# A state-space block and a product-key expert layer on one core: three more scaled rows on TensorE, and the stages dealt out anew

## The chip, the cores and the metric

The kernel runs on one core of one Trainium2 chip, in fp32. The metric is device time in microseconds of the whole program, median of three runs. Engines are named PE (TensorE), DVE (VectorE), ACT (ScalarE), POOL (GpSimd) and SP (SyncE).

## The reference

4096 tokens of width 512 go through two layers, each added to its input and layer-normed.

```python
x = _layernorm(x + attn(x))     # a Mamba-2 block
x = _layernorm(x + ffn(x))      # a product-key expert layer

# attn: u @ W_in -> z, xBC, dt; causal conv of 4 taps and silu; then
y, _ = ssd(x * dt[..., None], A * dt, B, C, 64)   # 16 heads of 64, state 128
y = (y + x * D) * silu(z)                         # x * D: the skip term
out = rmsnorm(y) * norm_scale @ W_out

# ffn: h = silu(x @ W_up.T + b_up) @ W_down.T + b_down   (512 -> 2048 -> 256)
sim = keys . (h @ W_q.T)                # 8 heads, 2 x 64 keys
scores, idx = top_k(sim, 8)             # then the 8 best of the 8 x 8 sums
indices                                 # 64 expert rows of each token
z = silu((h . down_embed[indices]) * softmax(sc))
out = sum over the 64 of z * up_embed[indices]
```

## The kernel before, in words

The tokens are 32 tiles of 128. For each tile every engine has an order written out by hand: a function `tile(i, first, ahead)` in the PE, ACT and DVE blocks. In one pass it does three things at once: the expert rows of tile i-1 that are left (`old`), the first expert rows of tile i (`new`), and the state-space block of tile i+1 (the calls under `ahead`), with the up, down and key projections of tile i between them. The engines meet only at semaphores.

**Expert rows.** One pick is one row of 768 numbers for each of the 128 tokens (256 of down_embed, 512 of up_embed). POOL gathers the 64 picks of a tile in order by indirect DMA (L275) into a ring of 13 slots; pick k+13 waits until pick k is used. The picks are in 22 groups, `GROUPS`; 0 to 3 are `new`, 4 to 21 `old`. For each pick DVE makes the dot with h (L1167), and ACT the coefficient by a Silu (L664). What then happens depends on the pick's letter. A `D` row is weighed by DVE (L1181), multiplied by its coefficient and added to a running sum, two groups later (`LAG`). A `P` row is scaled by ACT into one of 4 buffers (L673, 128x512) and added on PE by four transposes that accumulate in a bank (L506). At the end of a tile ACT copies this bank (`sum_out`, L681), PE turns it back (L514) and DVE adds it to its own sum (L1212) and norms it.

**The stages that the change moves.** On ACT: `xbc_copy` (L689), `inputs` (L701, L704: the three parts of the turned projection, each with a first tap), `turn_x1` (L793: the copy of the transposed x1, for which the up projection waits), `up_copy` and `up_silu` (L800, L806), `conv_silu` (L710), `masked_steps` (L726), `gates` (L736), `decays` (L741 to L750), `soft_exp` (L816), `skip_term` (L717: 8 scalings by D, which PE's y_diag waits for), `end_decay` (L758: xdec, for which DVE's scan output and PE's state_in wait), `state_decay` (L766), `turn_y` (L775), `gated_squares` and `gated_rms` (L780, L784), `back_sqrt` (L820) and `deviation` (L789). On PE: `up_proj` (L463), `turn_up` (L470), `down_proj` (L479), `z_proj` (L360), `y_off` (L397), `y_diag` (L413, L416), `turn_y` (L432), `out_proj` (L442) and `turn_back` (L514). On DVE: `convolve` (L1012), `private` (L1085: the vector h), `top_half`, `find_half` (L1091, L1097), `find_pairs` (L1124), `numbers` (L1146, which gives POOL its indices), `scaled_x` and `masked_products` (L1020 to L1029), `scan_out` (L1038) and `residual` (L1068, which waits for the last of out_proj by `op_mm`).

## Time and profile before

| | us |
|---|---|
| median of three runs (lowest, highest) | 3131.76 (3126.43, 3133.64) |
| the profiled execution | 3120.3 |
| its span, first to last instruction | 3118.5 |
| DVE busy in the span | 2770.7 |
| PE busy | 2628.5 |
| ACT busy | 2325.9 |
| POOL busy (2048 gathers) | 2062.9 |
| weighings on DVE, L1181 (1312 in the main form) | 988.0 |
| scaled rows on ACT, L673 (672 = 32 x 21) | 446.8 |

The span holds a start before the first tile, 32 tiles and an end in which the last tile's rows are used. Shares of busy time are means over stretches with different limits. An engine's idle time counts where another waits for it, so the rows of one tile in order of time tell more than the sums. The mean granted TensorE clock is 0.931 of full speed, where 1.00 is 2.4 GHz.

### The profile page before, as it was taken

What the parts mean: (1) busy time and instruction counts of PE and PEld (TensorE: products, weight loads), DVE (VectorE), ACT (ScalarE), POOL (GpSimd) and SP (SyncE); (2) the same over time, 40 slices, a digit from 0 to 9 for tenths busy, and PEclk for the clock granted to TensorE, in tenths of its full rate; (3) what the DMA queues carried; (4) which work ended last, traced back from release to release, by engine and by line L of the source; (5) the groups of instructions that cost most, each with busy time, mean ns of one, the idle gap of its engine ahead of it and who ended that gap; (6) DMA issues with size and microseconds to landing.
All of it is one profiled execution on the core that took longest, in us unless ns stands there. A gap on an engine that the chain in (4) does not pass through costs nothing.

```text
span 3118.5 us, 42958 instructions
## 1 busy us (share of the span) xinstructions
PE 2628.5 (84%) x10688; PEld 1613.2 (52%) x10688; DVE 2770.7 (89%) x10160; ACT 2325.9 (75%) x6674; POOL 2062.9 (66%) x2056
## 2 busy tenths in 40 slices
PE   7988888888888888888888888889888888888862
PEld 4455555555555555555555555555555555555531
DVE  3489899989999999999999999999999998999986
ACT  3477887777887777787777788777788777788753
POOL 0067676666676676676667667667667666667676
PEclk9999999999999999999999999999999999999975
DMA  8078888888888888888888888888888888888897
GB/s 284 26 264 279 283 285 268 280 291 279 279 289 273 273 299 280 281 289 269 268 296 281 281 285 282 263 281 294 282 279 289 272 275 292 279 278 290 271 310 271
DMA packets 189850, 856.65 MB, mean 275 GB/s; under 512 B 36192, under 2 KB 39392, under 8 KB 189088
## 3 DMA queue, kind: packets, MB, share of 16 engines
q0 software_dynamic: 163840, 805.44, 77.0%
q1 hardware_dynamic: 19104, 34.87, 3.2%
q10 hardware_dynamic: 6656, 13.60, 1.2%
q8 instruction: 85, 1.39, 0.2%
q14 instruction: 165, 1.35, 0.1%
HBM read 845.38 MB, written 8.39 MB: 274 GB/s over the span
## 4 chain that ended last, share of the span: by engine, by line
DVE 35%; PE 33%; ACT 11%; issue 9%; DMA 6%; POOL 6%; POOLq 0%; ACTq 0%; DVEq 0%; SPq 0%
PE bank L463 15%; DVE ring L1167 9%; DVE bank L1181 9%; PE bank L479 7%; POOL ring L275 6%; DMA ring<-embed,idx 6%; PE bank L338 3%; DVE i L1097 3%; ACT xc L704 3%; DVE v L1091 2%; DVE xdt L1138 2%; ACT scaled L673 2%; PE bank L470 2%; ACT coef L664 2%; DVE place L1124 1%
## 5 line engine op out<-in xcount | busy, mean ns | idle before, releaser
L275 POOL DMA_INDIRECT ring<-embed,idx x2048 | 2061.6, 1007 | 1040.9 <-issue 517.0
L1181 DVE SCALAR_TENSOR_TENSOR bank<-ring,coef,bank 128x512 f32<-128x512 f32 x1312 | 988.0, 753 | 8.8 <-ACT coef L664 1.4
L1167 DVE SCALAR_TENSOR_TENSOR ring<-ring,hcur 128x256 f32<-128x256 f32 x2048 | 815.4, 420 | 58.0 <-DMA ring<-embed,idx 55.7
L664 ACT ACTIVATE coef<-prob,zp 128x1 f32<-128x1 f32 x2048 | 455.6, 293 | 237.0 <-DVE ring L1167 235.8
L463 PE MATMUL bank<-w_up,zs 128*128 128x512 f32 x1024 | 509.4, 650 | 97.5 <-ACT zs L793 93.9
L506 PE MATMUL bank<-cst,scaled 128*128 128x128 f32 x2688 | 410.9, 305 | 171.9 <-ACT scaled L673 171.8
L506 PEld LDWEIGHTS bank<-cst,scaled 128*128 128x128 f32 x2688 | 351.2, 159 | 245.9 <-ACT scaled L673 213.3
L673 ACT ACTIVATE scaled<-ring,coef 128x512 f32<-128x512 f32 x672 | 446.8, 714 | 10.4
L463 PEld LDWEIGHTS bank<-w_up,zs 128*128 128x128 f32 x1024 | 206.6, 210 | 335.4 <-issue 233.9
L1012 DVE SCALAR_TENSOR_TENSOR xc<-raw,taps,xc 128x128 f32<-128x128 f32 x960 | 265.5, 348 | 90.7 <-ACT xc L704 90.6
L338 PE MATMUL bank<-w_in,ut 128*128 128x512 f32 (+1 forms) x768 | 289.7, 528 | 47.1 <-ACT seg L689 47.1
L800 ACT ACTIVATE h<-bank 128x512 f32<-128x512 f32 x128 | 76.4, 597 | 246.3 <-PE bank L463 246.3
L442 PE MATMUL bank<-w_out,xdec 128*128 128x512 f32 x512 | 252.6, 639 | 4.3 <-ACT xdec L775 4.3
L338 PEld LDWEIGHTS bank<-w_in,ut 128*128 128x128 f32 x768 | 142.0, 191 | 184.9 <-issue 108.1
L360 PE MATMUL bank<-w_in,ut 128*128 128x512 f32 x512 | 228.0, 599 | 4.4 <-ACT xc L704 4.4
L479 PE MATMUL bank<-w_down,seg 128*128 128x256 f32 x1024 | 231.6, 379 | 0.0
L479 PEld LDWEIGHTS bank<-w_down,seg 128*128 128x128 f32 x1024 | 189.6, 190 | 23.1
L1167 DVE DVE_READ_ACCUMULATOR ring<-ring,hcur 128x1 f32 x2048 | 171.3, 84 | 0.0
L360 PEld LDWEIGHTS bank<-w_in,ut 128*128 128x128 f32 x512 | 98.3, 192 | 128.5 <-issue 128.5
L442 PEld LDWEIGHTS bank<-w_out,xdec 128*128 128x128 f32 x512 | 102.6, 213 | 113.0 <-issue 105.1
L806 ACT ACTIVATE seg<-bank,bup 128x128 f32<-128x128 f32 x512 | 145.8, 373 | 14.2 <-PE bank L470 14.2
L726 ACT ACTIVATE seg<-cst,cur 128x128 f32<-128x128 f32 x512 | 155.6, 391 | 0.0
(150 smaller groups left out, 3764.4 us busy)
## 6 DMA issues: line engine op xcount, KB each, us to landing
ring<-embed,idx POOLq DMA_INDIRECT x2048, 4.6
ring<-uT SPq DMA_DIRECT2D x4, 2048.0 KB, 14.3
ut<-uT SPq DMA_DIRECT2D x32, 256.0 KB, 6.7
zs<-u SPq DMA_DIRECT2D x32, 256.0 KB, 6.2
out<-acc SPq DMA_DIRECT2D x32, 256.0 KB, 5.0
w_up<-W_upT ACTq DMA_DIRECT2D x1, 4096.0 KB, 12.8
w_in<-W_in ACTq DMA_DIRECT2D x1, 2560.0 KB, 17.2
w_in<-W_in ACTq DMA_DIRECT2D x1, 2048.0 KB, 21.7
```

What stands on the lines that cost most here:

```text
L275: pool.indirect_dma_start(out=ring[:, k % RING, :], out_offset=None, in_=embed, in_offset=bass.IndirectOffsetOnAxis(ap=idx[:, half, k:k + ...
L338: m = pe.matmul(bank[XR_BANKS[part]][:, 0:hi - lo], uT_v[:, k, :], w_in[:, k, DI + lo:DI + hi], start=(k == 0), stop=(k == KD - 1))
L360: m = pe.matmul(bank[Z_BANKS[b]][:, :], uT_v[:, k, :], w_in[:, k, b * BANK:(b + 1) * BANK], start=(k == 0), stop=(k == KD - 1))
L442: m = pe.matmul(bank[OP][:, :], yT[:, c * P:(c + 1) * P], w_out[:, c, :], start=(c == 0), stop=(c == KX - 1))
L463: m = pe.matmul(bank[UP_BANKS[b]][:, :], x1T[:, k, :], w_up[:, k, b * BANK:(b + 1) * BANK], start=(k == 0), stop=(k == KD - 1))
L479: m = pe.matmul(bank[DOWN][:, 0:DP], h1T[:, c, :], w_down[:, c, :], start=(c == 0), stop=(c == KU - 1))
L506: m = pe.matmul(bank[SUM][:, c * P:(c + 1) * P], scaled[:, (NPR * t + n) % BUFS, c * P:(c + 1) * P], ident, start=(n == 0 and c == 0), sto ...
L664: m = act.activation(coef[:, k:k + 1], prob_v[:, k:k + 1], ACT.Silu, scale=zp[:, k:k + 1])
L673: act.activation(scaled[:, n % BUFS, :], ring[:, k % RING, DP:ROW], ACT.Copy, scale=coef[:, k:k + 1])\
L1012: m = dve.scalar_tensor_tensor(out=xc[:, c, :], in0=raw[:, c, j:j + P], scalar=taps[:, c, j:j + 1], in1=xc[:, c, :], op0=ALU.mult, op1=ALU ...
L1167: m = dve.scalar_tensor_tensor(out=ring[:, k % RING, 0:DP], in0=ring[:, k % RING, 0:DP], scalar=1.0, in1=hcur[:, :], op0=ALU.mult, op1=ALU ...
L1181: dve.scalar_tensor_tensor(out=total if n == len(DVE_ROWS) - 1 else running[:, :], in0=ring[:, k % RING, DP:ROW], scalar=coef[:, k:k + 1], ...
```

## The change

`GROUPS` has 24 letters P instead of 21, in other places. On all three engines stages and groups change places. `gates` becomes `gate`, one call for each half, and `skip_term` waits for `hist_ok` too. The table of groups, and PE's part:

```diff
-GROUPS = ("DD", "PPPD", "DD", "DDD", "PPD", "DDD", "DD", "DDD", "PDDD", "DDD", "DDD", "DDDD", "PDD", "PPPD", "PP", "PDD", "PPPP", "D", "DDD", "PPPD", "D", "PDD")
+GROUPS = ("DD", "PPPD", "DD", "DDD", "PPD", "DDD", "PD", "DDD", "PDDD", "DDD", "DDD", "PDDD", "PDD", "PPPD", "PP", "PD", "PPPPD", "D", "PDD", "PPPPD", "D", "DD")
...
                     turn_xbc(i + 1, False, 0)
                     turn_xbc(i + 1, False, 1)
                     turn_xbc(i + 1, False, 2)
+                old(4, 5)
                 turn_x1(i)
-                old(4, 5, 6)
+                old(6)
                 up_proj(i, 0, first, ahead)
                 up_proj(i, 1, first, ahead)
+                old(7)
                 turn_up(i, 0)
                 up_proj(i, 2, first, ahead)
                 turn_up(i, 1)
-                old(7, 8)
                 up_proj(i, 3, first, ahead)
                 turn_up(i, 2)
+                old(8)
                 down_proj(i, 0, first, ahead)
+                old(9, 10)
                 turn_up(i, 3)
-                old(9)
                 down_proj(i, 1, first, ahead)
-                old(10)
                 down_proj(i, 2, first, ahead)
                 down_proj(i, 3, first, ahead)
+                old(11)
                 turn_h(i, ahead)
-                old(11, 12)
+                old(12)
                 key_scores(i, 0)
                 key_scores(i, 1)
                 if ahead:
                     z_proj(i + 1, 0)
+                old(13)
+                if ahead:
                     z_proj(i + 1, 1)
-                old(13)
-                if ahead:
                     step_sums(i + 1, 0)
                     step_sums(i + 1, 1)
                     step_sums(i + 1, 2)
                     step_sums(i + 1, 3)
                     turn_x(i + 1)
-                old(14, 15)
+                old(14, 15, 16, 17)
                 if ahead:
                     y_off(i + 1, False)
-                old(16, 17)
-                if ahead:
                     y_diag(i + 1, False, 0)
+                old(18)
+                if ahead:
                     y_diag(i + 1, False, 1)
-                old(18, 19)
+                old(19, 20, 21)
                 if ahead:
                     state_in(i + 1)
                     turn_y(i + 1)
-                old(20, 21)
-                if ahead:
                     out_proj(i + 1, False, 0)
+                new(0)
                 if not first:
                     turn_back(i - 1)
-                new(0)
+                new(1, 2, 3)
                 if ahead:
                     out_proj(i + 1, False, 1)
-                new(1, 2, 3)
```

ACT's part:

```diff
             def skip_term(i):
 
                 act.wait_ge(xc_ok, i + 1)
+                act.wait_ge(hist_ok, i + 1)
                 for c in range(KX):
...
                     xbc_copy(i + 1, 1)
                     xbc_copy(i + 1, 2)
                     inputs(i + 1, 0)
-                old(5)
+                old(5, 6)
+                turn_x1(i)
                 if ahead:
                     inputs(i + 1, 1)
-                turn_x1(i)
-                old(6)
-                if ahead:
                     inputs(i + 1, 2)
-                save_x1(i, first)
                 old(7)
                 up_copy(i, 0)
                 old(8)
+                up_silu(i, 0)
+                save_x1(i, first)
                 up_copy(i, 1)
-                up_silu(i, 0)
+                up_silu(i, 1)
                 up_copy(i, 2)
-                up_silu(i, 1)
                 old(9)
                 up_copy(i, 3)
                 up_silu(i, 2)
...
                 turn_h(i)
                 if ahead:
                     masked_steps(i + 1, range(0, NH // 4), False)
+                    conv_silu(i + 1)
                     masked_steps(i + 1, range(NH // 4, NH // 2), False)
                     masked_steps(i + 1, range(NH // 2, 3 * NH // 4), False)
                 old(13)
                 if ahead:
-                    conv_silu(i + 1)
                     masked_steps(i + 1, range(3 * NH // 4, NH), False)
-                    gates(i + 1, False)
-                old(14, 15)
+                old(14)
+                if ahead:
+                    gate(i + 1, False, 0)
+                    gate(i + 1, False, 1)
+                old(15)
                 if ahead:
                     decays(i + 1, False)
                 soft_exp(i)
+                old(16)
                 if ahead:
                     skip_term(i + 1)
-                old(16, 17)
+                old(17)
                 if ahead:
                     end_decay(i + 1, range(NH // 2))
-                old(18, 19)
+                old(18)
                 if ahead:
                     end_decay(i + 1, range(NH // 2, NH))
+                old(19)
+                if ahead:
+                    state_decay(i + 1, range(NH // 2))
                 old(20, 21)
                 hand_over(i, first)
                 if ahead:
-                    state_decay(i + 1, range(NH // 2))
+                    turn_y(i + 1)
+                    gated_squares(i + 1)
                     state_decay(i + 1, range(NH // 2, NH))
-                    turn_y(i + 1)
+                new(0)
                 if not first:
                     sum_out(i - 1)
-                new(0, 1)
-                if ahead:
-                    gated_squares(i + 1)
+                new(1, 2)
+                if ahead:
                     gated_rms(i + 1)
-                new(2)
                 if not first:
                     back_sqrt(i - 1)
+                new(3)
                 if ahead:
                     deviation(i + 1)
-                new(3)
```

DVE's part:

```diff
                 if ahead:
                     convolve(i + 1, 0, 1)
                     convolve(i + 1, 0, 2)
-                    convolve(i + 1, 1, 0)
                     time_steps(i + 1)
                 old(8)
                 if ahead:
+                    convolve(i + 1, 1, 0)
                     convolve(i + 1, 1, 1)
-                old(9, 10)
+                old(9)
                 if ahead:
                     convolve(i + 1, 1, 2)
                     convolve(i + 1, 2, 0)
                     convolve(i + 1, 2, 1)
-                old(11, 12)
+                old(10, 11, 12)
+                if ahead:
+                    convolve(i + 1, 2, 2)
                 private(i, first)
                 old(13)
-                if ahead:
-                    convolve(i + 1, 2, 2)
                 top_half(i, 0)
+                find_half(i, 0)
                 top_half(i, 1)
                 old(14)
                 pair_sums(i)
                 top_pairs(i)
                 old(15)
-                find_half(i, 0)
-                shifted(i)
                 find_half(i, 1)
                 find_pairs(i)
                 old(16)
+                shifted(i)
                 places(i)
                 old(17)
                 picked(i)
                 numbers(i)
                 if ahead:
                     scaled_x(i + 1)
+                old(18)
+                if ahead:
                     masked_products(i + 1)
-                old(18, 19, 20, 21)
+                old(19, 20, 21)
                 if ahead:
                     scan_out(i + 1, 0)
                     scan_out(i + 1, 1)
```

Three places of the order, each of the kernel before and then of the changed one, in a tile of the steady stretch.

ACT from `soft_exp` (L816) on, groups 16 to 19 of the old rows; `coef` are coefficients, `scaled` the P rows, `raw<-xc,dcol` the skip term (L717, in the changed kernel L718), `xdec` end_decay. Before:

```order
L816 ACTIVATE raised<-raised 128x64
L717 ACTIVATE raw<-xc,dcol 128x128 x8
L664 ACT_TABLE_LOAD
L664 ACTIVATE coef<-prob,zp 128x1 x4
L673 ACTIVATE scaled<-ring,coef 128x512 x4
L664 ACTIVATE coef<-prob,zp 128x1
L758 ACTIVATE xdec<-xdt,decay 128x64 x8
L664 ACTIVATE coef<-prob,zp 128x1 x7
L673 ACTIVATE scaled<-ring,coef 128x512 x3
L758 ACTIVATE xdec<-xdt,decay 128x64 x8
L664 ACTIVATE coef<-prob,zp 128x1 x4
L673 ACTIVATE scaled<-ring,coef 128x512
```

Changed:

```order
L816 ACTIVATE raised<-raised 128x64
L664 ACT_TABLE_LOAD
L664 ACTIVATE coef<-prob,zp 128x1 x5
L673 ACTIVATE scaled<-ring,coef 128x512 x4
L718 ACTIVATE raw<-xc,dcol 128x128 x8
L664 ACTIVATE coef<-prob,zp 128x1
L758 ACTIVATE xdec<-xdt,decay 128x64 x8
L664 ACTIVATE coef<-prob,zp 128x1 x3
L673 ACTIVATE scaled<-ring,coef 128x512
L758 ACTIVATE xdec<-xdt,decay 128x64 x8
L664 ACTIVATE coef<-prob,zp 128x1 x5
L673 ACTIVATE scaled<-ring,coef 128x512 x4
```

The skip term went behind the coefficients and scaled rows of group 16, and the second half of end_decay in front of those of group 19; group 18 has a scaled row, group 19 has four.

ACT at the start of a tile, around the copy of x1T; `raw` and `xc` are `inputs`, `zs<-bank` (L793) is the copy of x1T. Before:

```order
L704 ACTIVATE xc<-bank,cbias,taps 128x128 x4
L664 ACTIVATE coef<-prob,zp 128x1 x3
L701 ACTIVATE raw<-bank 128x4x128
L704 ACTIVATE xc<-bank,cbias,taps 128x128 x4
L793 ACTIVATE zs<-bank 128x512
L664 ACTIVATE coef<-prob,zp 128x1 x2
L701 ACTIVATE raw<-bank 128x2x128
L704 ACTIVATE xc<-bank,cbias,taps 128x128 x2
L833 ACTIVATE x<-xdt 128x512
```

Changed:

```order
L701 ACTIVATE raw<-bank 128x4x128
L704 ACTIVATE xc<-bank,cbias,taps 128x128 x4
L664 ACTIVATE coef<-prob,zp 128x1 x5
L673 ACTIVATE scaled<-ring,coef 128x512
L793 ACTIVATE zs<-bank 128x512
L701 ACTIVATE raw<-bank 128x4x128
L704 ACTIVATE xc<-bank,cbias,taps 128x128 x4
L701 ACTIVATE raw<-bank 128x2x128
L704 ACTIVATE xc<-bank,cbias,taps 128x128 x2
```

The copy of x1T went in front of the second part of `inputs`, and behind the coefficients and one scaled row of group 6; save_x1 (L833) left this stretch.

PE at the end of a tile: `out_proj` (L442) in two halves, `turn_back` (L514), the P rows of group 1 (L506), and the next tile's projection (L338). Before:

```order
L426 MATMUL bank<-xdec,bcb 128x512 x2
L432 MATMUL bank<-cst,xdt 128x128 x8
L506 MATMUL bank<-cst,scaled 128x128 x4
L442 MATMUL bank<-w_out,xdec 128x512 x4
L514 MATMUL bank<-cst,turned 128x128 x4
L442 MATMUL bank<-w_out,xdec 128x512 x4
L506 MATMUL bank<-cst,scaled 128x128 x12
L338 MATMUL bank<-w_in,ut 128x512 x8
```

Changed:

```order
L506 MATMUL bank<-cst,scaled 128x128 x16
L426 MATMUL bank<-xdec,bcb 128x512 x2
L432 MATMUL bank<-cst,xdt 128x128 x8
L442 MATMUL bank<-w_out,xdec 128x512 x4
L514 MATMUL bank<-cst,turned 128x128 x4
L506 MATMUL bank<-cst,scaled 128x128 x12
L442 MATMUL bank<-w_out,xdec 128x512 x4
L338 MATMUL bank<-w_in,ut 128x512 x8
```

The three P rows of group 1 went in front of the second half of out_proj.

## Rows read from the trace of the kernel before

**Rows 1.** The page, part 1: busy us of each engine and its share of the span.

```profile
PE 2628.5 (84%) x10688; PEld 1613.2 (52%) x10688; DVE 2770.7 (89%) x10160; ACT 2325.9 (75%) x6674; POOL 2062.9 (66%) x2056
```

**Rows 2.** The page, part 4: shares of the chain that ended last, by engine.

```profile
DVE 35%; PE 33%; ACT 11%; issue 9%; DMA 6%; POOL 6%; POOLq 0%; ACTq 0%; DVEq 0%; SPq 0%
```

**Rows 3.** Source line L1085: count, ns min/median/max, first and last start.

```profile
L1085 DVE TENSOR_TENSOR h<-bank,bdown x32: 410/425/425, 142.9 to 2995.2; 128x256 f32<-128x256 f32 x32
```

**Rows 4.** DVE in order of time: start us, us, line, operation, [idle before, releaser].

```profile
1637.92 2.29 DVE L1029 TENSOR_TENSOR seg<-seg,bcb 128x2048 f32<-128x2048 f32 x1
...
1648.15 1.29 DVE L1038 TENSOR_TENSOR xdt<-bank,decay 128x512 f32<-128x512 f32 x2 [0.29 <-issue]
...
1659.75 0.42 DVE L1167 SCALAR_TENSOR_TENSOR ring<-ring,hcur 128x256 f32<-128x256 f32 x1 [0.53 <-DMA ring<-embed,idx]
...
1664.16 0.75 DVE L1068 SCALAR_TENSOR_TENSOR xdt<-bank,sm,zs 128x512 f32<-128x512 f32 x1
...
1676.78 1.14 DVE L1012 SCALAR_TENSOR_TENSOR xc<-raw,taps,xc 128x128 f32<-128x128 f32 x4 [2.81 <-ACT xc L704]
...
1679.18 0.75 DVE L1181 SCALAR_TENSOR_TENSOR bank<-ring,coef,bank 128x512 f32<-128x512 f32 x1
1679.85 0.42 DVE L1167 SCALAR_TENSOR_TENSOR ring<-ring,hcur 128x256 f32<-128x256 f32 x1
...
1704.32 0.42 DVE L1085 TENSOR_TENSOR h<-bank,bdown 128x256 f32<-128x256 f32 x1 [1.81 <-PE bank L479]
```

**Rows 5.** Groups by line and shape, 1000 to 2014 us: busy us, mean ns, idle before.

```profile
L1181 DVE SCALAR_TENSOR_TENSOR bank<-ring,coef,bank 128x512 f32<-128x512 f32 x448 | 337.4, 753 | 3.4 <-ACT coef L664 0.9
L673 ACT ACTIVATE scaled<-ring,coef 128x512 f32<-128x512 f32 x228 | 151.6, 714 | 3.6
L506 PE MATMUL bank<-cst,scaled 128*128 128x128 f32 x912 | 136.1, 301 | 33.3 <-ACT scaled L673 33.3
```

**Rows 6.** ACT in order of time, middle and start of a tile.

```profile
1632.45 2.45 ACT L717 ACTIVATE raw<-xc,dcol 128x128 f32<-128x128 f32 x8
1634.92 1.28 ACT L664 ACT_TABLE_LOAD   x1
...
1637.10 2.56 ACT L673 ACTIVATE scaled<-ring,coef 128x512 f32<-128x512 f32 x4
...
1646.06 2.00 ACT L758 ACTIVATE xdec<-xdt,decay 128x64 f32<-128x64 f32 x8
...
1677.17 0.61 ACT L701 ACTIVATE raw<-bank 128x512 f32<-128x512 f32 x1
...
1679.02 0.65 ACT L793 ACTIVATE zs<-bank 128x512 f32<-128x512 f32 x1
```

**Rows 7.** POOL in order of time, the gathers.

```profile
1638.09 2.95 POOL L275 DMA_INDIRECT ring<-embed,idx  x1 [3.42 <-ACT scaled L673]
...
1646.56 0.94 POOL L275 DMA_INDIRECT ring<-embed,idx  x1 [0.30 <-issue]
```

**Rows 8.** PE in order of time, end and start of a tile.

```profile
1658.81 3.60 PE L442 MATMUL bank<-w_out,xdec 128*128 128x512 f32 x8
...
1679.72 8.60 PE L463 MATMUL bank<-w_up,zs 128*128 128x512 f32 x16 [3.12 <-ACT zs L793]
```

**Rows 9.** The end of the last tile, all engines in order of time.

```profile
3113.33 0.69 DVE L1212 TENSOR_TENSOR acc<-acc,bank 128x512 f32<-128x512 f32 x1 [2.21 <-PE bank L514]
```

**Rows 10.** Windows: us, PE, PEld, DVE, ACT, POOL busy (x), granted clock, DMA share, GB/s.

```profile
170.00:172.00 2.00, 0.00 (x1) 0.00 (x0) 2.00 (x5) 1.10 (x5) 1.70 (x2) 1.00 0.95 323
...
174.00:176.00 2.00, 2.00 (x4) 0.96 (x3) 2.00 (x8) 1.99 (x6) 1.70 (x2) 0.50 0.84 270
...
1676.60:1679.60 3.00, 0.00 (x1) 0.00 (x0) 2.82 (x10) 3.00 (x11) 2.02 (x3) 0.95 0.88 287
1679.80:1682.40 2.60, 2.60 (x3) 1.09 (x4) 2.60 (x10) 2.27 (x9) 1.99 (x3) 0.50 0.97 317
```

More of the change, by code:

```diff
@@ L557, in tile @@
                     z_proj(i + 1, 0)
-                    z_proj(i + 1, 1)
                 old(13)
                 if ahead:
+                    z_proj(i + 1, 1)
                     step_sums(i + 1, 0)
@@ L565, in tile @@
                     turn_x(i + 1)
-                old(14, 15)
+                old(14, 15, 16, 17)
                 if ahead:
                     y_off(i + 1, False)
-                old(16, 17)
+                    y_diag(i + 1, False, 0)
+                old(18)
                 if ahead:
-                    y_diag(i + 1, False, 0)
                     y_diag(i + 1, False, 1)
-                old(18, 19)
+                old(19, 20, 21)
                 if ahead:
@@ L728, in masked_steps, with gate @@
                         m.then_inc(am_ok, 1)
-            def gates(i, first):
-                for b in range(2):
-                    act.wait_ge(z_mm, 2 * i + b + 1)
-                    if b == 0 and not first:
-                        act.wait_ge(sim_mm, 2 * i)
-                    act.activation(zs[:, b * BANK:(b + 1) * BANK], bank[Z_BANKS[b]][:, :], ACT.Silu).then_inc(z_ok, 1)
+            def gate(i, first, b):
+                act.wait_ge(z_mm, 2 * i + b + 1)
+                if b == 0 and not first:
+                    act.wait_ge(sim_mm, 2 * i)
+                act.activation(zs[:, b * BANK:(b + 1) * BANK], bank[Z_BANKS[b]][:, :], ACT.Silu).then_inc(z_ok, 1)
             def decays(i, first):
@@ L919, in _ @@
             conv_silu(0)
-            gates(0, True)
+            gate(0, True, 0)
+            gate(0, True, 1)
             act.dma_start(w_up[:, :, :], W_upT.rearrange("(k p) n -> p k n", p=P)).then_inc(w_up_in, 16)
```

## The prediction

> **What bounds the kernel now.** I read the page's totals first. DVE is busy 89% of the span, PE 84%, ACT 75% and POOL 66% [rows 1]: none is full, so the second view is the chain that ended last. It gives DVE 35%, PE 33%, ACT 11%, DMA 6% and POOL 6% [rows 2]. The reader should see that the bound changes hands inside a tile. L1085 (the private vector h) starts 32 times from 142.9 to 2995.2 us [rows 3], so a tile takes (2995.2 - 142.9) / 31 = 92.0 us. I then followed the tile from 1612 to 1704 us on all engines.
>
> From L1085 to the scan output (L1038), DVE is never idle for more than a few tenths; DVE and ACT set the time there. From L1038 to the end of the tile, DVE leads and its rows arrive just in time. From the first transposed input to the next L1085, PE leads: DVE waits 2.81 us for ACT at L1012 and 1.81 us for PE at L1085 [rows 4]. So DVE work taken out **before** L1085 is worth nothing; work taken out behind it, or a shorter ACT/PE chain before it, is.
>
> **The change, part by part.**
>
> *Three rows more on PE.* Each takes one weighing from DVE, 753 ns as recorded [rows 5], and 0.67 us from its start to that of the dot behind it (1679.18 to 1679.85; the dot takes the 0.34 to 1680.19) [rows 4]. Group by group DVE loses a weighing in groups 6, 11, 15 and 18 and gains one in 16. Weighings run two groups late: that of 6 falls in group 8, in front of L1085, and goes into the wait. The others lie between L1085 and L1038: 2 x 0.67 = 1.3 us saved. ACT pays 3 x 0.714 us and PE 3 x (136.1 / 228) = 3 x 0.60 us a tile [rows 5]. With 75% and 84% busy [rows 1] both have the room as a sum; the question is where.
>
> *Last part of the convolution in front of L1085.* The two instructions of 0.52 us leave the DVE-bound stretch and go into the 1.81 us wait [rows 4]. Saved: 0.5 us, at no cost while that wait lasts.
>
> *Skip term behind group 16.* Before, ACT does the skip term (2.45 us), loads a table (1.28 us) and only then makes the coefficients and four scaled rows of group 16 [rows 6]; POOL, with all 13 slots taken, stands 3.42 us for the first of them [rows 7]. Now these rows come 2.45 us earlier, minus 0.2 for a fifth coefficient, and gathers restart about 2.3 to 3 us earlier. That pays at the 0.53 us wait for a row behind L1038 [rows 4]: it goes. The skip term now ends late, near 1639, but y_diag also waits for the masked products of DVE. Those move behind group 18 (3 dots and a weighing, 1.7 us) and, with 1.8 us saved before them, end where they did (1640.1). y_diag started at 1641.1: nothing is lost. What would be late next, if the skip slipped 1.5 us, is y_diag.
>
> *Second half of end_decay in front of the coefficients of group 19.* Before, DVE was held at L1038 until ACT's second L758, which runs from 1646.06 to 1648.06 [rows 4, 6]. Now it ends near 1644.7, but the coefficients of 19, which DVE needs for a weighing in group 21, come behind it. ACT's work from the end of soft_exp (now about 0.8 us earlier, at 1631.6, since z_proj, group 13 and the gates are dealt out anew): 1.28 + 5 x 0.21 + 4 x 0.65 + 2.45 + 0.2 + 1.9 + 3 x 0.21 + 0.7 + 1.95 + 5 x 0.21 = 13.8 us, so 1645.4. DVE alone would be at that weighing at 1644.8; it waits 0.6 to 0.9 us, then does 0.67 + 0.34. The scan starts at 1646.7 instead of 1648.15: **-1.4 us**, not the -2.3 that DVE's own work and waits (0.67 x 2, 0.5, 0.5) would give.
>
> *Contention of the masked products.* The gather that runs beside L1029 takes 2.95 us where others take 0.95 [rows 4, 7]. It did so once per tile and will again; it moves to another row of the ring. The Trainium skill (GPSIMD Engine Reference, the table of the overview) says that GpSimd shares SBUF interfaces with VectorE and contends with DVE instructions that have two SBUF inputs. The trace agrees, with 2.95 against 0.95 us. By bounds: 0 if it only moves, 2.0 us of POOL if a second gather is hit. I take 0: with 0.94 + 0.30 us a gather [rows 7] POOL needs 64 x 1.25 + 4 = 84 us of a tile of 90.
>
> *End of the tile.* With the 0.53 us wait gone DVE is 1.9 us ahead when the last new group is done. But out_proj's second half now stands behind new(1) on PE. ACT finishes scaled rows of group 1 at about 1659.3; 0.4 us of transposes and 3.45 us of out_proj [rows 8] give op_mm at 1663.3. DVE would want it at 1662.2 and waits 1.1 us: L1068 starts at 1663.4 instead of 1664.16 [rows 4]. So **-0.7 us** are left here of the 1.9. Bounds: -1.9 (no wait) and +2.7 (all of this out_proj at the low clock, +3.4). I take the value at full clock, as its row is.
>
> *ACT's copy of x1T in front of inputs(1).* Before, inputs(1) stood in front of it, 1.85 us from 1677.17 to 1679.02 [rows 6]. Now, instead: two coefficients and one scaled row of group 6 with a pause for the coefficients, 0.4 + 0.05 + 0.65 = 1.1. The up projection starts **0.7 us** earlier against this tile's own start. What waits for inputs(1), the convolution on DVE, has three dots and three weighings in front of it (3.0 us): covered.
>
> *Moves at no cost:* find_half, shifted and time_steps are the same work on one engine, and save_x1 and up_silu stay inside the 3.44 us that PE takes per up_proj. Table loads stay as many.
>
> **The sum.** -0.7 at the end of the tile and -0.75 in front of up_proj: 1.45 us a tile, over the 30 tiles that have both an old and a next one, 43.5 us. The last tile's end is paced by gathers, but with two DVE rows last, the 2.21 us wait for turn_back [rows 9] goes: 2.2 us. Together 46 us: 3120.3 - 46 = 3074 for the profiled execution, whose span is 3118.5. The median of three is 11.5 us above that execution, so 3132 - 46 = **3086**.
>
> **Rivals.**
>
> *A: the clock stays up in up_proj.* Before, PE idles 3.12 us and up_proj's first 16 records take 8.60 us [rows 8], where the same at 3.44 per 8 would take 6.9: granted clock 0.95 on the mean of the gap, then 0.50 (the 1.2 GHz level) [rows 10]. Now the gap is about 2.0 us, 0.44 us of transposes (group 6) and 0.1. In tile 0 a gap of 2.1 us around 171 was followed by a granted clock of 0.50 at 174, when PE was busy again [rows 10]; so a shorter gap is no safety. If it stays at 1.00, PE gains 1.7 more, and DVE, which had 1.81 us of wait there, becomes the bound after some 1.0: 2.4 to 2.6 us a tile, 3132 - 30 x 2.5 - 2 = 3055.
>
> *B: slower, through out_proj behind new(1).* Between out_proj's halves PE now gets turn_back and three rows at ACT's pace, 1.7 us of work in 4.5 us. If the clock falls there, out_proj's second half takes 5.1 to 6.9 us; L1068 is 1.7 to 3.4 us later and xbc_proj behind it too. The gain of 1.45 us a tile is gone from 1.45 us of delay on. At 1.7 to 3.4: +0.2 to +2.0 us a tile, 3136 to 3190, mostly 3150. For it: the clock fell behind 2.1 us of gap in tile 0 with PE busy again. Against: no single gap here is over 1.2 us.
>
> *C: little gained.* ACT is late in the groups 16 to 19 by another microsecond, or rows of group 13 come late with a shorter tile: 0 to 0.5 us a tile, 3115 to 3132.
>
> *D: table loads cost more where they change place.* The load of 1.28 us at 1634.92 and four coefficients of 0.21 fill the time to the scaled row at 1637.10 [rows 6]: 1.28 + 0.84 = 2.12 of 2.18, so the load has no time beside its own. Now two loads stand between back_sqrt and deviation; at 1.28 us they end at 1664.9, just before the variance is ready. If each cost 1.4 us more, deviation and norm1 would be 2.4 us late: +1.0 us a tile net, 3160. The Trainium skill (ScalarE: Activation LUTs, What ACT_TABLE_LOAD costs) gives 1283 ns and about 1380 ns of drain, 2.66 us for every switch. The trace agrees with the first figure (1.28) and shows no drain.
>
> **How the numbers follow.** Forecast 0.46; A 0.28; B 0.12; C 0.12; D 0.02. A measurement here tells about 0.2% (6 us) from no change. Slower by more takes B mostly and D: 0.13; within 0.2% takes half of C: 0.07; faster 0.80. The range reaches from A with its bounds (3050) to the small gains of C (3125); outside lie B, D and the last of C, and a little below A.
>
> **What would show it.** Each step has its sign: DVE weighings 43 to 40 a tile; POOL's 3.42 us wait under 2; a wait at L1038 gone but a new one of 0.6 to 0.9 at a weighing for coef (L664); DVE waiting about 1 us for PE at L1068; up_proj's idle of 3.12 down to two pieces; L1085 starting every 90.5 us. Wrong: a tile of 92 us or more, L1085 waiting on PE for over 2 us with up_proj at full clock, or out_proj's second half over 5 us.

## The result, and the profile after

| | before | after |
|---|---|---|
| median us (lowest, highest) | 3129.72 (3126.43, 3133.64) | 3039.11 (3032.93, 3045.77) |
| profiled execution, its span | 3120.3, 3118.5 | 3037.97, 3036.0 |
| mean granted clock | 0.931 | 0.963 |

Four runs of each. The ratio is 0.9714, 95% [0.9695, 0.9733]: faster by 90.6 us where 46 were forecast, and beyond the range. In the changed kernel L1068, L1085, L1181 and L1212 are L1073, L1090, L1186 and L1217; L717 is L718, and L463, L442, L673 and L793 keep their numbers.

Page, parts 1 and 5, of the kernel after, to lay beside [rows 1]. Columns of part 5: count, busy us, mean ns, idle before and its releaser.

```profile
PE 2629.5 (87%) x11072; PEld 1605.0 (53%) x11072; DVE 2707.0 (89%) x10064; ACT 2391.8 (79%) x6770; POOL 2082.2 (69%) x2056
...
L463 PE MATMUL bank<-w_up,zs 128*128 128x512 f32 x1024 | 465.0, 602 | 1.6 <-issue 1.6
```

The same group (up_proj) on the page of the kernel before:

```profile
L463 PE MATMUL bank<-w_up,zs 128*128 128x512 f32 x1024 | 509.4, 650 | 97.5 <-ACT zs L793 93.9
```

DVE did 96 instructions less in 64 us less, PE and ACT more, as moved. L463 took 602 ns each; before it took 650 and 97.5 us of idle stood in front of it. The transposes of group 6 now stand in that idle time.

Source line of the private vector, after:

```profile
L1090 DVE TENSOR_TENSOR h<-bank,bdown x32: 408/414/425, 139.0 to 2914.2; 128x256 f32<-128x256 f32 x32
its engine sat idle before it (us, times) until:
  PE bank L479: 18.1, 6
```

A tile takes (2914.2 - 139.0) / 31 = 89.5 us, where [rows 3] gave 92.0: 77.1 us of the span. The first h comes 3.9 us earlier, and the stretch behind the last start is 1.5 us shorter (121.8 for 123.3): 82.5 in all, the difference of the spans. The private vector found PE late 6 times; before, 31 times and 71.9 us.

The table gives the mean offset of a step behind the start of h, over the 12 tiles between 1000 and 2200 us, read from the timelines of both kernels.

| start of | before | after | moved | forecast |
|---|---|---|---|---|
| scan output (L1038 / L1043) | 36.15 | 34.50 | -1.65 | -1.4 |
| residual (L1068 / L1073) | 52.20 | 51.45 | -0.75 | -0.7 |
| copy of x1T (L793) | 67.09 | 65.63 | -1.46 | -1.45 |
| up_proj (L463) | 67.79 | 66.27 | -1.52 | -1.45 |
| first turn_up (L470) | 76.52 | 73.37 | -3.15 | -1.45 |
| next h | 92.69 | 90.02 | -2.67 | -1.45 |

Up to the up projection it went as the sum says. Then its first two blocks take 7.11 us instead of 8.74, a gain of 1.63 more, and DVE, now the last in front of h, keeps 0.5 of that. That is rival A. The means hide two kinds of tiles: the residual starts at 50.8 in 8 of the 12, at 52.7 to 53.5 in 3 and at 52.0 in one.

The middle of a tile, DVE, after (h at 1572.17), in order of time: start us, us, line, operation, idle before and its releaser.

```profile
1605.63 0.76 DVE L1186 SCALAR_TENSOR_TENSOR bank<-ring,coef,bank 128x512 f32<-128x512 f32 x1 [0.62 <-ACT coef L664]
...
1606.64 1.28 DVE L1043 TENSOR_TENSOR xdt<-bank,decay 128x512 f32<-128x512 f32 x2
...
1624.16 0.75 DVE L1073 SCALAR_TENSOR_TENSOR xdt<-bank,sm,zs 128x512 f32<-128x512 f32 x1
...
1637.62 1.14 DVE L1017 SCALAR_TENSOR_TENSOR xc<-raw,taps,xc 128x128 f32<-128x128 f32 x4 [3.71 <-ACT xc L704]
```

The new 0.62 us wait for a coefficient, between the bounds 0.6 and 0.9 of the forecast, is there (8.0 us in 11 tiles, 0.73 each). This tile is the one with its residual at 52.0 (1624.16 - 1572.17). ACT and POOL of the same tile:

```profile
1592.06 1.28 ACT L664 ACT_TABLE_LOAD   x1
1593.36 1.04 ACT L664 ACTIVATE coef<-prob,zp 128x1 f32<-128x1 f32 x5
1594.43 2.56 ACT L673 ACTIVATE scaled<-ring,coef 128x512 f32<-128x512 f32 x4
1596.89 2.44 ACT L718 ACTIVATE raw<-xc,dcol 128x128 f32<-128x128 f32 x8
...
1602.66 2.01 ACT L758 ACTIVATE xdec<-xdt,decay 128x64 f32<-128x64 f32 x8
```

```profile
1595.42 0.94 POOL L275 DMA_INDIRECT ring<-embed,idx  x1 [1.16 <-ACT scaled L673]
...
1599.21 2.09 POOL L275 DMA_INDIRECT ring<-embed,idx  x1 [0.30 <-issue]
```

POOL's wait of 3.42 us [rows 7] is 1.16, and one gather is still stretched beside the masked products (L1034, from 1598.19), to 2.09 us.

PE, after: the start of up_proj in an ordinary tile, then in one of the few tiles whose up projection is long. The idle time in front is the same.

```profile
1548.13 0.66 PE L506 MATMUL bank<-cst,scaled 128*128 128x128 f32 x4 [1.88 <-ACT scaled L673]
1548.63 7.13 PE L463 MATMUL bank<-w_up,zs 128*128 128x512 f32 x16
```

```profile
1185.22 0.66 PE L506 MATMUL bank<-cst,scaled 128*128 128x128 f32 x4 [1.88 <-ACT scaled L673]
1185.72 8.82 PE L463 MATMUL bank<-w_up,zs 128*128 128x512 f32 x16
```

Windows of those two up projections: us, busy of PE, PEld, DVE, ACT, POOL, granted clock, DMA share, GB/s.

```profile
1548.70:1551.80 3.10, 3.10 (x9) 1.43 (x9) 3.10 (x11) 3.10 (x11) 2.33 (x3) 1.00 0.86 260
1185.80:1189.00 3.20, 3.20 (x6) 1.41 (x6) 3.20 (x12) 3.20 (x11) 2.44 (x3) 0.57 0.86 281
```

The first line is at 2.4 GHz, the second for the most part at 1.2. I counted this through the program, by the time from up_proj's first record to the first turn_up (7.0 us at full clock, 8.3 and more with a low one): 29 of 31 tiles are long before, 4 of 31 after. The idle time in front is 3.12 us in 29 tiles before, also in the two that are not long, and 1.88 us in 29 tiles after, also in the four that are.

### The profile page after: what moved, and what is told of

The parts are those of the page before. It is cut to its first block, busy times and chain, and to the rows that moved or that the text cites. A ratio compares the mean times of both kernels' runs of the same rounds, so it can differ in the third digit from the quotient of the medians.

```text
span 3036.0 us, 43854 instructions
## 1 busy us (share of the span) xinstructions
PE 2629.5 (87%) x11072; PEld 1605.0 (53%) x11072; DVE 2707.0 (89%) x10064; ACT 2391.8 (79%) x6770; POOL 2082.2 (69%) x2056
## 4 chain that ended last, share of the span: by engine, by line
PE 33%; ACT 24%; DVE 20%; issue 10%; POOL 7%; DMA 7%; ACTq 0%; SPq 0%; DVEq 0%; POOLq 0%
POOL ring L275 7%; PE bank L360 7%; DMA ring<-embed,idx 6%; DVE bank L1186 6%; PE bank L506 6%; DVE xc L1017 5%; ACT scaled L673 4%; DVE ring L1172 4%; ACT coef L664 4%; ACT xdec L758 4%; PE bank L494 4%; PE bank L338 3%; PE bank L442 3%; PE bank L463 3%; ACT raw L718 2%
## 5 line engine op out<-in xcount | busy, mean ns | idle before, releaser
L1186 DVE SCALAR_TENSOR_TENSOR bank<-ring,coef,bank 128x512 f32<-128x512 f32 x1216 | 910.6, 749 | 26.4 <-ACT coef L664 21.3
L506 PE MATMUL bank<-cst,scaled 128*128 128x128 f32 x3072 | 485.6, 301 | 273.4 <-ACT scaled L673 272.6
L506 PEld LDWEIGHTS bank<-cst,scaled 128*128 128x128 f32 x3072 | 379.8, 154 | 366.9 <-ACT scaled L673 349.9
L673 ACT ACTIVATE scaled<-ring,coef 128x512 f32<-128x512 f32 x768 | 513.6, 716 | 12.5
L463 PE MATMUL bank<-w_up,zs 128*128 128x512 f32 x1024 | 465.0, 602 | 1.6 <-issue 1.6
L338 PE MATMUL bank<-w_in,ut 128*128 128x512 f32 (+1 forms) x768 | 289.0, 526 | 38.5 <-ACT seg L689 38.5
L463 PEld LDWEIGHTS bank<-w_up,zs 128*128 128x128 f32 x1024 | 189.3, 192 | 207.2 <-issue 205.1
L442 PE MATMUL bank<-w_out,xdec 128*128 128x512 f32 x512 | 240.4, 613 | 8.1 <-ACT xdec L775 8.1
L338 PEld LDWEIGHTS bank<-w_in,ut 128*128 128x128 f32 x768 | 143.4, 190 | 190.8 <-issue 122.5
L1172 DVE DVE_READ_ACCUMULATOR ring<-ring,hcur 128x1 f32 x2048 | 163.2, 80 | 0.0
L442 PEld LDWEIGHTS bank<-w_out,xdec 128*128 128x128 f32 x512 | 95.2, 196 | 111.7 <-issue 96.6
L416 PE MATMUL bank<-xdt,seg 128*128 128x64 f32 x1024 | 133.3, 262 | 0.0
```

Source lines behind the costliest of these rows:

```text
L338: m = pe.matmul(bank[XR_BANKS[part]][:, 0:hi - lo], uT_v[:, k, :], w_in[:, k, DI + lo:DI + hi], start=(k == 0), stop=(k == KD - 1))
L442: m = pe.matmul(bank[OP][:, :], yT[:, c * P:(c + 1) * P], w_out[:, c, :], start=(c == 0), stop=(c == KX - 1))
L463: m = pe.matmul(bank[UP_BANKS[b]][:, :], x1T[:, k, :], w_up[:, k, b * BANK:(b + 1) * BANK], start=(k == 0), stop=(k == KD - 1))
L506: m = pe.matmul(bank[SUM][:, c * P:(c + 1) * P], scaled[:, (NPR * t + n) % BUFS, c * P:(c + 1) * P], ident, start=(n == 0 and c == 0), sto ...
L673: act.activation(scaled[:, n % BUFS, :], ring[:, k % RING, DP:ROW], ACT.Copy, scale=coef[:, k:k + 1])\
L1172: m = dve.scalar_tensor_tensor(out=ring[:, k % RING, 0:DP], in0=ring[:, k % RING, 0:DP], scalar=1.0, in1=hcur[:, :], op0=ALU.mult, op1=ALU ...
```

## The experiments

Theory T: the gain is rival A's on top of the forecast's (clock 1.6 - 0.5, path 1.5 a tile). Rivals: it is the three rows alone, or the new order alone, whatever the clock does. "Long" below is the count of tiles with a long up projection. All times are medians with the interval of the ratio to the kernel before, which was measured again beside each group of runs: its median was 3129.15 beside order_only, rows_only, before_fill and after_p6_late, 3124.88 beside skip_early, end_late, out_early and x1_late, and 3128.14 beside the other four. Offsets behind h are means over all tiles that lie between 1000 and 2200 us, as in the table above. Where transposes of an expert row stand between up_proj's first two blocks and turn_up (after_p6_late, x1_late), full clock gives 7.4 us.

### The order without the rows, and the rows without the order

order_only is the changed kernel with the old `GROUPS` (21 P); rows_only is the kernel before with the new `GROUPS` (24 P), each engine in its old order.

```diff
# order_only, against the changed kernel (rows_only is the reverse line in the kernel before)
-GROUPS = ("DD", "PPPD", "DD", "DDD", "PPD", "DDD", "PD", "DDD", ...)
+GROUPS = ("DD", "PPPD", "DD", "DDD", "PPD", "DDD", "DD", "DDD", ...)
```

> The changed kernel with the table of groups of before: 21 scaled rows on PE, the new order of stages. Theory (clock and shorter ACT/PE path in front of up_proj, DVE-bound elsewhere): group 6 has no scaled row, so the copy of x1T comes about 0.7 us earlier still, the gap in front of up_proj is under 2.2 us and the clock stays at 1.00; DVE gets three weighings of 0.67 us back, 2 us a tile, of which some go into the wait at the private vector. Tile 91.0 to 91.8 us, 3070 to 3100 us. Rival (the rows are the change, the order only makes room for them): 3115 to 3130 us.

Measured: 3145.44, ratio 1.0053 [1.0033, 1.0074]: slower by half a per cent, and missed.

> The kernel before with the new table of groups: 24 scaled rows, the old order. PE then has the scaled row of group 6 in front of up_proj while ACT makes it behind the copy of x1T, so up_proj starts 0.8 us later. Theory: DVE's 2 us a tile are lost to that and to the clock, which still falls in a gap of 3 us or more: 3110 to 3150 us. Rival (DVE's work is what counts): three weighings less, 2 us a tile, 3060 to 3075 us.

Measured: 3208.05, ratio 1.0263 [1.0242, 1.0284]: much slower, and missed.

Neither half gains: +16 and +79 us, and together -90. In rows_only the row of group 6 comes on ACT behind inputs(1) and the copy of x1T, and on PE in front of up_proj. PE, rows_only:

```profile
1634.56 1.11 PE L506 MATMUL bank<-cst,scaled 128*128 128x128 f32 x4 [4.24 <-ACT scaled L673]
1635.47 8.26 PE L463 MATMUL bank<-w_up,zs 128*128 128x512 f32 x16
```

Up_proj starts 70.81 us behind h (before 67.79), as much later as a tile is longer (94.96 us for 92.01), and the clock still falls in it: all 31 tiles are long (8.1 to 9.3 us). In order_only the clock is up (1 long, the last), but DVE, with three rows more, reaches the scan output 1.0 us later than in the changed kernel (35.50) and the residual 2.65 us later (54.10). More than DVE's own rows stands there: the new order puts ACT's `turn_y` in front of the second half of state_decay, and ACT stands at it. Source line L775, order_only:

```profile
L775 ACT ACTIVATE xdec<-bank x64: 591/597/599, 88.0 to 2979.5; 128x512 f32<-128x512 f32 x64
its engine sat idle before it (us, times) until:
  PE bank L432: 110.8, 36
```

In the kernel before the same wait is 1.7 us. To test it, order_state takes order_only and puts that half back in front.

```diff
+                    state_decay(i + 1, range(NH // 2, NH))
                     turn_y(i + 1)
                     gated_squares(i + 1)
-                    state_decay(i + 1, range(NH // 2, NH))
```

> The new order with the old 21 scaled rows (3145 us), and the second half of state_decay in front of turn_y and gated_squares on ACT again, as before the change. Theory: with 43 rows to weigh DVE reaches the scan late, ACT's turn_y waits 3.6 us for it, and DVE then waits 2.1 us for state_decay behind turn_y; taken out of that row the wait goes: -2 us a tile, 3080 to 3095 us. Rival (DVE's three rows more are the whole loss): 3135 to 3150 us.

Measured: 3111.93 (3106.48 to 3118.49), ratio 0.9942 [0.9924, 0.996]: a miss, between the two ranges, with 33 us come back. The 68.3 us that DVE waited at new_state for state_decay are gone, new_state moves from 46.18 to 44.34 us behind h (after: 43.45), and the wait at L775 goes from 110.8 to 62.7 us. So this part of the new order needs the rows: with DVE late, ACT stands in the middle. With this one part put back, the rest of the new order is 16 us faster than the kernel before without the rows; that the order as a whole depends on them is not shown.

### The clock in the up projection

before_fill is the kernel before with 20 transposes of the identity into a free bank in front of up_proj (extra work, nothing left out). They change nothing but what PE does in its wait; the last tile, which has no next one, gets none.

```diff
+            def fill(i):
+                pe.wait_ge(xr_ok, 3 * i + 6)
+                pe.wait_ge(st_ok, 2 * i + 2)
+                for c in range(20):
+                    pe.transpose(bank[UP_BANKS[0]][:, (c % 4) * P:(c % 4 + 1) * P], ident, ident)
...
                 old(4, 5, 6)
+                if ahead:
+                    fill(i)
                 up_proj(i, 0, first, ahead)
```

> The kernel before with 20 transposes of the identity on PE (about 2.2 us) in the 3.1 us gap in front of up_proj, into a bank that up_proj then overwrites; nothing else changed. Theory (the clock in up_proj is worth 1.7 us a tile, and DVE has 1.8 us of wait there): the granted clock stays at 1.00, the 16 first records take 7.0 us instead of 8.6, 30 x 1.4 to 1.7 us less: 3078 to 3090 us. Rival (clock indifferent, or transposes do not hold it): 3125 to 3135 us.

Measured: 3081.74 (3080.9 to 3083.29), ratio 0.9855 [0.9836, 0.9875], a hit. PE and a window of before_fill; the line of the up projection is L469 there:

```profile
1655.31 2.35 PE L457 MATMUL bank<-cst 128*128 128x128 f32 x20
1658.59 7.13 PE L469 MATMUL bank<-w_up,zs 128*128 128x512 f32 x16 [0.94 <-ACT zs L801]
```

```profile
1658.70:1662.00 3.30, 3.30 (x8) 1.51 (x9) 3.30 (x13) 2.24 (x9) 2.37 (x3) 1.00 0.83 259
```

None of the 30 tiles with the transposes is long; the last, without them, took 7.60 us. Up_proj starts where it did (67.81 us behind h, before 67.79), so no path is shorter. The clock alone is worth 47 us, 1.5 a tile, to the kernel before (39 us between the two profiled executions). With the transposes in the gap it stays at 1.00. The Trainium skill (TensorE: Matmul & The Clock Gate, Part 4: PE-mode transpose) says that a transpose doesn't count as PE-busy in the same way, and that the full clock doesn't engage for it. These fp32 transposes do hold the clock, so the rows do not agree, and the measurement decides.

before_x1 makes the gap short in the kernel before by the copy of x1T alone.

```diff
+                turn_x1(i)
                 if ahead:
                     inputs(i + 1, 1)
-                turn_x1(i)
```

> The kernel before with one part of the change alone: ACT's copy of x1T in front of the second part of the inputs. Theory: the gap in front of up_proj shrinks from 3.1 to 1.3 us, up_proj starts 1.85 us earlier and runs at full clock (7.0 us for 16 records), together 3.4 us on PE; DVE had 1.8 us of wait at the private vector and is then the bound: -1.6 to -1.8 us a tile, 3065 to 3080 us. Rival (this copy hands on only its own 1.85 us and the clock still falls): the same gain but with up_proj at 8.6 us.

Measured: 3082.82, ratio 0.9859 [0.9839, 0.9879], 3 us over the expectation. The gap is 1.23 us, and 1 tile is long, the last. An earlier up projection and a higher clock together gave no more than the clock alone in before_fill: DVE is now the last in front of h (it waits there for PE once, in before_fill 28 times) and takes the rest.

The next two lengthen the gap in the changed kernel: after_p6_late moves PE's row of group 6 behind the first up projection, x1_late moves it behind the second, and puts the copy of x1T behind inputs(1) again.

```diff
# after_p6_late, PE
-                old(6)
                 up_proj(i, 0, first, ahead)
+                old(6)
                 up_proj(i, 1, first, ahead)
```

```diff
# x1_late, ACT
-                old(5, 6)
-                turn_x1(i)
+                old(5)
                 if ahead:
                     inputs(i + 1, 1)
+                turn_x1(i)
+                old(6)
+                if ahead:
                     inputs(i + 1, 2)
```

> The changed kernel with PE's transposes for the scaled row of group 6 behind the first up_proj instead of in front of it; ACT and DVE as in the changed kernel. Theory A (those 0.44 us in the gap hold the clock): the gap of 2.5 us is empty, the granted clock falls to 0.50 in up_proj, the 16 records take 8.6 us again; of the 1.7 us DVE hides 0.5: +1.2 us a tile, 3070 to 3080 us. Theory B (the shorter gap holds it, whatever is in it): no difference, 3032 to 3046 us.

Measured: 3056.22 (3050.84 to 3061.8), ratio 0.9769 [0.9744, 0.9794]: between the two ranges. Not all tiles do the same: 14 of 31 are long, 17 at full clock.

> The changed kernel with ACT's copy of x1T behind the second part of the inputs again, and PE's row of group 6 behind the second up_proj. Theory: the copy comes 0.7 us later, PE's gap is 3.1 us and empty, the clock falls in every tile (8.6 us for up_proj's first 16 records): up_proj's second part ends 2.4 us later, DVE hides 0.5 of it: +1.9 us a tile, 3088 to 3105 us. Rival (the clock does not depend on this gap): +0.7, less what DVE hides: 3040 to 3060 us.

Measured: 3092.89 (3085.63 to 3102.91), ratio 0.9897 [0.9871, 0.9923]: a hit in time, but by 19 long tiles with longer ones among them (10.3 us), not by all 31. So the order on ACT and the work left in PE's gap are worth 54 us of the 91.

### Other parts taken back, one at a time

All three start from the changed kernel.

```diff
# skip_early, ACT
+                if ahead:
+                    skip_term(i + 1)
                 old(16)
-                if ahead:
-                    skip_term(i + 1)
                 old(17)
```

> The changed kernel with the skip term in front of the coefficients of group 16 again, nothing else. Theory: ACT's sum up to the coefficients of group 19 is the same, but the scaled rows of group 16 come 2.45 us later, y_off stands behind them on PE, y_diag ends about 0.8 us behind the point where DVE wants it, and POOL stands 2.4 us longer for its slot: +0.8 to +1.5 us a tile, 3060 to 3085 us. Rival (ACT's sum is what counts, its order is not): 3030 to 3048 us.

Measured: 3099.97, ratio 0.991 [0.9894, 0.9927]: 61 us are lost, more than I put on it. POOL stands again; POOL of skip_early:

```profile
1443.27 0.94 POOL L275 DMA_INDIRECT ring<-embed,idx  x1 [3.81 <-ACT scaled L673]
```

y_off comes 2.8 us later (28.81 for 26.03), the scan output 1.8 us later (36.32), and 16 tiles are long. The long tiles are a second loss which I had not counted, and these runs do not explain it: PE's idle time in front of up_proj is the same 1.9 us, with the same four transposes behind it, as in the changed kernel. One of the long tiles of skip_early:

```profile
1484.61 0.66 PE L506 MATMUL bank<-cst,scaled 128*128 128x128 f32 x4 [1.86 <-ACT scaled L673]
1485.11 8.82 PE L463 MATMUL bank<-w_up,zs 128*128 128x512 f32 x16
```

```diff
# end_late, ACT
                 old(18)
+                old(19)
                 if ahead:
                     end_decay(i + 1, range(NH // 2, NH))
-                old(19)
-                if ahead:
                     state_decay(i + 1, range(NH // 2))
```

> The changed kernel with the second half of end_decay behind the coefficients and four scaled rows of group 19 again. Theory: the scan output waits for it as before the change; it ends 5.65 us behind the rows of group 18 on ACT instead of 1.95, and the scan starts 1.7 us later: +1.2 to +1.7 us a tile, 3073 to 3092 us. Rival (the rows of group 19 on PE and POOL are worth as much as the scan): 3030 to 3048 us.

Measured: 3092.22, ratio 0.9891 [0.9874, 0.9907], at the upper end. The scan output is at 36.41, the residual at 53.38: both 1.9 us late. It has only 7 long tiles, so most of its loss is path. (Its out_proj also runs in part at the low clock, in every tile read; the residual still falls back by no more than the scan output.)

```diff
# out_early, PE
-                new(1, 2, 3)
                 if ahead:
                     out_proj(i + 1, False, 1)
+                new(1, 2, 3)
```

> The changed kernel with the second half of out_proj in front of the new groups 1 to 3 on PE again. In the changed kernel the residual starts at 50.8 us behind the private vector, in three tiles of twelve at 52.7 to 53.5, where this half ran 4.7 us instead of 3.6. Theory (the residual waits for it by 0.8 us, and the sparse rows in front of it now and then let the clock fall): -0.8 to -1.3 us a tile, 3000 to 3016 us. Rival (the gap moves behind xbc_proj's second part, 2.3 us and more, and the clock falls there): 3030 to 3050 us.

Measured: 3031.98 (3026.99 to 3033.85), ratio 0.9697 [0.9681, 0.9713]: as the rival had it. Against the changed kernel's own 0.9714 [0.9695, 0.9733] that can't be told apart. The residual does come 0.7 us earlier (50.73), but the copy of x1T only 0.2 (65.41). The rival's reason is in the trace too: PE now stands longer in front of xbc_proj's third part, and in 5 of 13 tiles the clock falls there. PE of such a tile, out_early:

```profile
1716.05 3.15 PE L338 MATMUL bank<-w_in,ut 128*128 128x256 f32 x8 [3.16 <-ACT seg L689]
```

At full clock this part takes 1.99 us. In these 5 tiles the copy of x1T starts at 66.0 to 67.2, in the other 8 at 64.2 to 65.6. So the place of out_proj was no gain of the change: what the other place gives, the clock takes.

### What stands in front of the up projection

In out_early ACT waits with a table loaded for DVE's dots of group 4, and only then copies xBC out for PE. ACT and PE, out_early:

```profile
1623.74 0.67 ACT L664 ACTIVATE coef<-prob,zp 128x1 f32<-128x1 f32 x3 [1.87 <-DVE ring L1172]
...
1625.68 1.06 ACT L689 ACTIVATE seg<-bank 128x512 f32<-128x512 f32 x2
1626.31 1.99 PE L338 MATMUL bank<-w_in,ut 128*128 128x256 f32 x8 [2.58 <-ACT seg L689]
```

PE's last part of xbc_proj needs the bank that the copy frees. copy_ab puts two of the three copies in front of group 4, copy_a only the first.

```diff
# copy_a, against out_early; copy_ab takes xbc_copy(i + 1, 1) along
+                if ahead:
+                    xbc_copy(i + 1, 0)
                 old(4)
                 if ahead:
-                    xbc_copy(i + 1, 0)
                     xbc_copy(i + 1, 1)
                     xbc_copy(i + 1, 2)
```

> For a version that beats both: out_early (3032 us), and ACT's first two copies of the projection in front of the coefficients of group 4. ACT waits there 1 to 2 us for DVE's dots, while PE waits for the first copy with its third projection. Theory: that projection follows on the second without a gap, the first inputs come 1.5 to 2 us earlier, DVE's wait of 3.4 us at the convolution shrinks by as much: -1 to -1.8 us a tile, 2978 to 3002 us. Rival (the scaled rows of group 4 come later, and PE and POOL wait for them): 3020 to 3045 us.

Measured: 2996.94 (2989.3 to 3001.95), ratio 0.9587 [0.9565, 0.9609], a hit.

> As copy_ab, but only the first copy in front of group 4. Theory: PE's third projection needs this copy alone, so it gains the same on PE, and the scaled rows of group 4 are 0.5 us earlier; the second copy and the inputs come no earlier than ACT is through with group 4: -0.3 to -1.2 us a tile, 2995 to 3022 us. Rival (no gain, since ACT's sum up to the inputs is the same): 3026 to 3034 us.

Measured: 2945.33 (2941.34 to 2948.85), ratio 0.942 [0.94, 0.944]: 50 us below the expectation, and faster than both kernels, by 94 us than the changed one. ACT, then PE, then the source line of h, all of copy_a:

```profile
1573.87 0.58 ACT L689 ACTIVATE seg<-bank 128x512 f32<-128x512 f32 x1
1574.47 1.28 ACT L664 ACT_TABLE_LOAD   x1
1577.13 0.67 ACT L664 ACTIVATE coef<-prob,zp 128x1 f32<-128x1 f32 x3 [1.38 <-DVE ring L1173]
```

```profile
1570.16 8.76 PE L338 MATMUL bank<-w_in,ut 128*128 128x512 f32 x24
```

```profile
L1091 DVE TENSOR_TENSOR h<-bank,bdown x32: 408/414/425, 138.7 to 2818.4; 128x256 f32<-128x256 f32 x32
```

The copy fills a time in which ACT waits anyway, and xbc_proj runs through in one stretch. In out_early ACT's third copy then also waits for PE's late third part; here that part is done when ACT comes to it, so the copy of x1T starts at 62.27 instead of 65.41, and a tile takes 86.4 us instead of 89.4. Part of this is the clock again: with no gap in xbc_proj it falls there in no tile of 13, where it did in 5 before (those 5 alone make 0.7 of the 3.1 us), and no up projection is long. How the rest divides between PE and ACT was not tested. DVE's wait for the inputs falls from 36.9 us in 11 tiles to 3.4 in 10. The second copy in front of group 4 (copy_ab) stops ACT until PE is that far, and holds up the coefficients: x1T at 63.81, and 7 tiles long.

## Why the prediction was wrong, and where it was right

**Right on the mean: the path.** The 0.7 us at the residual measured 0.75, the 0.75 in front of up_proj 0.77, their sum 1.52 where 1.45 was forecast. That the first fits so well is in part luck: in 8 of 12 tiles the residual is at 50.8, 1.4 us earlier than before, and in 3 it is later than before, by rival B, which the sum had at nothing. DVE's wait for PE at the residual was forecast at about 1 us and is 0.6 on the mean (7.0 us in 11 tiles; 0.63 in the tile below).

```profile
1533.75 0.75 DVE L1073 SCALAR_TENSOR_TENSOR xdt<-bank,sm,zs 128x512 f32<-128x512 f32 x1 [0.63 <-DVE sm L1069]
```

The releaser named had long been done; out_proj's second half ends there. The scan output gained 1.65 (forecast 1.4) with the coefficient wait at its forecast size. That these are the right causes is borne out by end_late and skip_early, where the scan output falls back by 1.9 and 1.8 us and the time by 53 and 61 us (in skip_early the clock has a share).

**Wrong: the step that kept the clock low in up_proj.** I put in the sum that up_proj takes as long as before, at 1.2 GHz, because one row of tile 0 showed the clock falling behind a gap of 2.1 us [rows 10], and gave rival A only 0.28. The runs show in its place a clock that stays up in 27 of 31 tiles, worth 1.63 us, of which DVE hides 0.5. With it rival A's 2.4 to 2.6 us a tile are the 2.5 measured over the program. before_fill shows the price by itself (47 us in the kernel before), and after_p6_late shows why one row was a poor witness: with the 0.44 us of transposes out of the gap, the same kernel does it either way, 14 tiles to 17. What decides for the single tile stays open: skip_early has the changed kernel's gap, transposes included, and 16 long tiles. The sum should have treated this place as a chance for each tile.

**Outside the sum.** The first h came 3.9 us earlier. I had counted 30 tiles and the tail only; no run here takes this apart. The tail: the 2.21 us wait of [rows 9] became 0.72, and 1.5 us were gained where I had 2.2. PE's and DVE's ends are nearer there than I put them.

```profile
3030.85 0.69 DVE L1217 TENSOR_TENSOR acc<-acc,bank 128x512 f32<-128x512 f32 x1 [0.72 <-PE bank L514]
```

**Rival B is real but not in most tiles.** In some tiles DVE waits for a gathered row, the coefficients of group 1 come late, and PE stands between out_proj's halves. DVE and PE of such a tile, after:

```profile
1254.97 0.42 DVE L1172 SCALAR_TENSOR_TENSOR ring<-ring,hcur 128x256 f32<-128x256 f32 x1 [1.55 <-DMA ring<-embed,idx]
...
1257.10 2.39 PE L506 MATMUL bank<-cst,scaled 128*128 128x128 f32 x12 [2.03 <-ACT scaled L673]
...
1259.29 4.64 PE L442 MATMUL bank<-w_out,xdec 128*128 128x512 f32 x8
```

Out_proj takes 4.64 us for 3.60, and the residual of such tiles is at 52.7 to 53.5 instead of about 51: 3 of the 12 tiles of the table. I gave it nothing in the sum; against full clock it costs 0.6 us a tile on the mean (51.45 for 50.8). out_early does not price it by itself, since there the clock falls in xbc_proj instead.

**Rivals C and D.** Nothing of C is seen. For D, the table loads (197 before and after) still take 1.28 us where they changed place, with the next ACTIVATE 0.02 us behind (1592.06 to 1593.36).

**What I missed altogether.** The three rows and the order are not terms that add. I costed them as such, and expected a gain of order_only (3070 to 3100) and little change of rows_only (3110 to 3150); both lose.

## What to carry to other kernels

Look at what the matmul engine does in the last microseconds before a long run of matmuls: at a gap near 2 us a small piece of other work in it, or a slightly earlier release, can decide over a fifth of the time of the first matmuls (7.0 or 8.7 us), though not in every tile. Test a hand-written order together with the split of work that it was made for, and not only each alone. Where an engine waits anyway, put in front of that wait the one small instruction that frees a bank for another engine: here one copy took the kernel from 3031.98 to 2945.33 us, nearly as much as the whole change.

## What the hardware did that I had not expected

The clock does not fall at one length of idle time; between the extremes it is a matter of the tile. The idle time is that of PE in front of up_proj in nearly all tiles. "Four transposes" are those of group 6, between the idle time and up_proj.

| kernel | PE's idle before up_proj, us | long tiles |
|---|---|---|
| before_fill | 0.94, transposes ahead of it | 0 of 30 |
| before_x1 | 1.23 | 1 of 31 |
| order_only | 1.60 | 1 of 31 |
| copy_a | 1.6, then four transposes | 0 of 31 |
| copy_ab | 1.8, then four transposes | 7 of 31 |
| out_early | 1.9, then four transposes | 1 of 31 |
| changed kernel | 1.88, then four transposes | 4 of 31 |
| end_late | 1.9, then four transposes | 7 of 31 |
| skip_early | 1.9, then four transposes | 16 of 31 |
| after_p6_late | 2.35 | 14 of 31 |
| x1_late | 3.11 | 19 of 31 |
| before | 3.12 | 29 of 31 |
| rows_only | 4.2, then four transposes | 31 of 31 |

The one long tile of before_x1, order_only and out_early is the last, whose order is another. Neither the step from 1 to 16 long tiles at the same 1.9 us, nor the difference between x1_late and before at the same gap, is explained by these runs. Each count is from one execution. Long tiles with a next one differ among themselves too (8.1 us in rows_only to 10.3 in x1_late), by where in up_proj the clock falls. This may also be what spreads the times of one kernel: the four times of the changed kernel lie 13 us apart, those of before_fill 2.4. It is not shown, since those of copy_a, with no long tile either, lie 7.5 apart.
